# Layer 0's attention: clip and exponential over two blocks of keys at once, weighted blocks written in a row

## What is computed

```python
kc = k.reshape(B, H, Nc, CHUNK, Dh)          # CHUNK = 128, Nc = 8
vc = v.reshape(B, H, Nc, CHUNK, Dh)
scores = jnp.einsum('bhnd,bhjcd->bhnjc', q, kc) / jnp.sqrt(jnp.asarray(Dh, dtype=q.dtype))
scores = jnp.clip(scores, -10.0, 10.0)
scores = jnp.where(mask == 0, jnp.asarray(-10.0, scores.dtype), scores)
attn = jax.nn.softmax(scores, axis=-1)       # over the 128 keys of one block
ctx = jnp.einsum('bhnjc,bhjcd->bhnd', attn, vc)
```

## Time and profile before

| | |
|---|---|
| median of 3 runs | 3406.07 us (3404.3 to 3408.29) |
| profiled execution | 3398.74 us |
| its span | 3397.1 us |
| busy share of PE, DVE, ACT, POOL | 70%, 72%, 44%, 61% |
| mean granted TensorE clock | 0.822 of full |

### The profile page before, as it was taken

One profiled execution on the slowest core, in us unless ns is written; L12 is line 12 of the kernel. 1 busy time (PEld: TensorE's weight loads), 2 busy tenths in 40 slices (PEclk: granted clock), 3 DMA queues, 4 the chain that ended last, 5 costly groups with the idle time before them and its releaser, 6 DMA issues. The chain is left out here.

```text
span 3397.1 us, 91971 instructions
## 1 busy us (share of the span) xinstructions
PE 2366.9 (70%) x32653; PEld 1654.5 (49%) x32988; DVE 2435.1 (72%) x5337; ACT 1499.6 (44%) x2211; POOL 2056.8 (61%) x1733
## 2 busy tenths in 40 slices
PE   4488878785435888888885638885647777777760
PEld 2266666564322554554554526774425555555550
DVE  3399999897665877777784546535768888888856
ACT  2355555552221444444342324442336666666650
POOL 2387878783222655555564325552239999989971
PEclk8688888886666999999997768886669988889885
DMA  6732233222543222122114531203421212112215
GB/s 215 255 92 69 68 73 79 68 55 48 158 146 110 55 54 55 45 51 55 43 43 113 163 120 58 79 20 102 123 89 57 70 53 68 55 54 68 62 41 124
DMA packets 259867, 285.00 MB, mean 84 GB/s; under 512 B 147889, under 2 KB 211953, under 8 KB 259457
## 3 DMA queue, kind: packets, MB, share of 16 engines
q1 hardware_dynamic: 254848, 262.48, 26.9%
q0 software_dynamic: 4608, 16.78, 1.4%
HBM read 183.52 MB, written 95.36 MB: 82 GB/s over the span
## 5 line engine op out<-in xcount | busy, mean ns | idle before, releaser
L314 POOL TENSOR_TENSOR xg<-xc 128x512 f16<-128x512 f32 x1536 | 1813.0, 1206 | 671.8 <-ACT xc L788 556.7
L1009 PE MATMUL ps<-vs,xc 128*128 128x33 bf16 (+1 forms) x13824 | 850.3, 189 | 176.6 <-DVE work L1348 89.5
L1009 PEld LDWEIGHTS ps<-vs,xc 128*128 128x128 bf16 x13824 | 683.1, 101 | 501.6 <-issue 258.1
L1009 PE MATMUL ps<-vs,xg 128*128 128x33 bf16 (+1 forms) x9216 | 779.0, 187 | 0.3 <-issue 0.3
L1009 PEld LDWEIGHTS ps<-vs,xg 128*128 128x128 f16 x9216 | 596.9, 99 | 3.7 <-issue 3.7
L1290 DVE CUSTOM_DVE_ANT_0 full<-ks,mask_n 128x1024 bf16<-128x1024 f32 x320 | 456.4, 1426 | 69.5 <-DVE xn L1385 28.1
L788 ACT ACTIVATE xc<-ps 128x512 f32<-128x512 f32 x512 | 305.7, 597 | 438.9 <-PE ps L953 438.8
L788 ACT ACTIVATE xc<-cv,lift 128x512 f32<-128x512 f32 x512 | 350.4, 718 | 291.4 <-DVE cv L1323 290.1
L1300 DVE CUSTOM_DVE_ANT_0 full<-ps,mask_n 128x512 bf16<-128x512 f32 x512 | 353.0, 689 | 169.3 <-DVE top L1300 62.0
L968 PE MATMUL ps<-qs,sel 128*128 128x512 f32 x640 | 424.3, 665 | 0.2 <-ACT ps L767 0.2
L788 ACT ACTIVATE xc<-cv,cols 128x512 f32<-128x512 f32 x320 | 231.3, 723 | 383.1 <-DVE cv L1331 374.5
(11 more groups left out here) (136 smaller groups left out, 3540.6 us busy)
## 6 DMA issues: line engine op xcount, KB each, us to landing
qs<-q_d SPq DMA_DIRECT2D x224, 128.0 KB
ks<-k_d SPq DMA_DIRECT2D x224, 128.0 KB
ks<-row_d SPq DMA_DIRECT2D x40, 512.0 KB
part<-row_d SPq DMA_DIRECT2D x40, 512.0 KB
v_d<-vbuf SPq DMA_DIRECT2D x24, 792.0 KB, 4.2
vs<-v_d SPq DMA_DIRECT2D x96, 198.0 KB
q_d<-part SPq DMA_DIRECT2D x32, 512.0 KB
k_d<-part SPq DMA_DIRECT2D x32, 512.0 KB
```

The lines of the kernel that those rows point to most:

```text
L314: eng.tensor_tensor(plo[:, r, :], prob[:, r, :], phi[:, r, :], ALU.subtract).then_inc(low_done(layer, u, s)[0], 1)
L1009: mm = pe.matmul(acc, half[:, r, it * P:(it + 1) * P], vs[:, n, at:at + width], start=opens and h == 0 and v == 0, stop=h == 1 and v == 1, ...
```

## The change

In layer 0, the clip, the mask and the exponential are done for two neighbouring tiles in one operation over 2 x 512 columns. `settle_two(s)`, for even s, waits for both scores and writes two slots of `arg`; `exp_two(s)` reads them and writes two slots of `prob`, and raises `s_exp` by 2. `s_p` now counts pairs in layer 0, and all counts against it are adjusted, as are PE's waits ahead of an even score. The order of PE's loop, its wait for `s_chfree`, POOL's operations and the place of `blocks_done` in DVE's loop stay.

`blk`, the view of `work` into which the multiplication writes and from which the reduction reads, is laid out anew: before, the block j was the fastest index (step of one element), after, j is the slowest (step of 128 elements) and the 128 results of a block lie in a row.

```diff
-        blk = work[:, :, :].rearrange("p t f -> p (t f)").rearrange("p (t d j) -> p j t d", d=32, j=BLOCKS)
+        blk = work[:, :, :].rearrange("p j (t d) -> p j t d", d=32)
...
             if layer == 0:
-                return u * (TILES * UNROLL) + s
+                return u * (TILES // 2 * UNROLL) + s // 2
...
+                    def exp_two(s):
+                        T, r = tile_value(s), s % DEEP
+                        act.wait_ge(s_p, p_at(s))
+
+                        act.wait_ge(s_av, T - DEEP + 2)
+                        act.activation(prob[:, r:r + 2, :], arg[:, r % RING:r % RING + 2, :], ACT.Exp,
+                                       scale=2.0 * CLIP, bias=lift[:, 0:1]).then_inc(s_exp, 2)
...
-                        exps(s)
+                        if layer:
+                            exps(s)
+                        elif s % 2 == 0:
+                            exp_two(s)
...
                             if layer == 0:
-                                if not (first and s < RING):
-                                    pe.wait_ge(s_p, T - CREDIT - RING + 1)
+                                if s % 2 == 0 and not (first and s < RING):
+                                    pe.wait_ge(s_p, settled_before(layer, u, s - RING) + 1)
                                 mm = pe.matmul(bank, ks[:, n, blk_j], qs[:, n, cut], start=True, stop=True)
...
+                    def settle_two(s):
+
+                        T, r = tile_value(s), s % RING
+                        c, j = s // BLOCKS % 2, s % BLOCKS
+                        dve.wait_ge(s_score, T - CREDIT + 2)
+                        dve.wait_ge(s_exp, T - RING + 2)
+                        dve.scalar_tensor_tensor(arg[:, r:r + 2, :], ps[:, r:r + 2, :], -0.5,
+                                                 mask_t[:, j:j + 2, c * HALF:(c + 1) * HALF], ALU.max, ALU.min
+                                                 ).then_inc(s_p, 1)
...
-                        if s < total and layer != 1 and s % RING not in RELU_AT[layer]:
+                        if layer == 0 and s < total and s % 2 == 0:
+                            settle_two(s)
+                        if layer > 1 and s < total and s % RING not in RELU_AT[layer]:
                             settle(s)
```

## The result

The changed kernel takes 3693.1 us (median; 3688.5 to 3694.7) against 3407.2 for the kernel before: ratio 1.0838, 95% interval 1.0825 to 1.0851. The forecast was 3654 with a range of 3600 to 3712. It is slower by 286 us where 248 were forecast. In the profiled execution the span is 3686.9 us, 289.8 more than before. The stage of layer 0's attention, from the first clip to the operation on the mask that follows the last reduction, went from 632 us (164.4 to 796.6) to 910 (166.3 to 1075.9), +277. What follows it went from 2600.5 to 2611.0, and the stage begins 2 us later.

The account below looks back on a forecast made before the run. DVE was taken to bound layer 0's attention, PE close; the change closes a loop between them. 251 pairs x 3.32 + 62 reductions x 0.54 = 867 us against 618, +248: 3654 us, range 3600 to 3712.

Parts of the forecast that it names:

- The wait for two scores (1): In layer 0, the odd score waits behind a weighing needing DVE's last multiplication: PE and DVE loop once a pair.
- PE's part of the loop: From multiplication's end through weighing and odd score to the clip: 1.26 us at full clock, 1.67 at half.
- Clip, multiplication (2, 3): On DVE: clip over 1024 columns 1.22 us, 1.14 until the reciprocal; multiplication with contiguous output 0.43 instead of 0.64.
- Rival C: Multiplication stays at 0.64 us, 53 us more, 3707; or reduction stays near 1.22, 3624; chance 0.09 for either.
- Reduction (4): DVE's reduction, now reading with a step of 128 elements, goes from 1.220 to 1.90 us, once in four pairs.
- excess over PE's part: DVE's 2.05 us around the reduction outlasts PE's path by 0.79 us at full or 0.38 at half clock.
- ACT and POOL (5): Merged exponential and POOL's subtractions end about 4.7 us after the clip began, needed after over 9: covered, priced at nothing.
- The sum (6): Layer 0's loop: 3.07 us a pair at full clock, 3.48 at half, 3.32 mixed; stage 867 us against 618.
- the mixed clock: TensorE in the loop at granted clock 0.70, 60% of the time at half clock: 3654 us, chance 0.56.
- rival B: The same PE and DVE loop at half clock throughout: 897 us for the pairs, +279, 3685 us; chance 0.14.
- Rival D: Odd score gets out ahead of the weighing, no loop binds, DVE's total decides: -27 us, 3379 us; chance 0.05.

Follow-up runs that it names:

- filler run: The changed kernel plus two unread products of 512 columns once a pair, ahead of PE's waiting weighing: 3632.5 us, ratio 1.0663 to the kernel before.

## Why the prediction was right, point by point

**The wait for two scores (1).** Right in mechanism and place. PE's part of the loop, worked out as 1.26 us at full and 1.67 at half clock, is 1.25 in the filler run and 1.62 here. The half-clock weighing took 0.59 when it came out of an idle stretch (505.65 to 506.24), not 0.64.

**Clip, multiplication (2, 3).** 1.22 and 1.14 until the reciprocal: measured 1.225 and 1.14. Multiplication 0.43: measured 0.424. Rival C, that it stays at 0.64, fell. The clip's line of the page, with the mean in ns and the idle before it:

```profile
L1329 DVE SCALAR_TENSOR_TENSOR cv<-ps,mask_t 128x1024 f32<-128x1024 f32 x256 | 313.5, 1225 | 333.9 <-PE ps L957 311.7
```

**Reduction (4).** 1.90 forecast from L1213, 1.968 measured; 0.07 short. The excess over PE's part was put at 0.38 at half clock and is 4.02 - 3.41 = 0.61: 0.07 from the duration, 0.05 because PE's part is shorter, and the rest from what lies around the reduction, 0.03 ahead and 0.22 behind, 0.25 where 0.15 had been taken.

**ACT and POOL (5).** Covered, as said: the run with the exponential alone is equal to before, and POOL is 56 to 59% busy in the windows from 200 to 1000 us, where near 60% was forecast.

**The sum (6), and the step that missed.** The full-clock pair was 3.07, measured 3.04; the half-clock pair 3.48, measured 3.41. What was wrong is "60% of the time at half clock", taken from projection stretches with PE 58 to 68% busy at 0.64 and 0.74. Here PE is 71 to 74% busy in every window of 100 us from 200 to 1000, more than in either, and the clock is 0.50 throughout. The filler run has the same busy share, 71.7%, and 0.91. So the busy share in the windows was no guide from one stage to another. PE's share itself was put at up to 70% and its idle stretch at 1.1 to 1.4 us; the profile shows 0.84, since it counts the last score to its end (0.77 us) and not to where the next product could start.

So the forecast's own choice, the mixed clock with a chance of 0.56, did not come true, and the range was right because it took in rival B, half clock throughout, with 0.14. B gave 3685 against 3693. Over the same 251 pairs that the sum counts, the traces have 618.4 us before and 892.2 after (first multiplication at 175.39, the one of iteration 510 at 1067.59), where B had 897 and the forecast 867. That B came so close is in part luck: its pair was 0.07 too long, 18 us in all, and its excess for the reduction 0.23 too short, 14 us.

The sentence "neither engine can run ahead, whatever the durations are" is borne out by the filler run: with the clock nearly full the loop is intact. Rival D, faster by DVE's total, failed at the point that was named for it. The runs with four banks show that its sum would have failed with the loop open as well. Like is compared with like there: four banks with the whole change take 3390.0 us, four banks without it 3379.3. The change costs 11 us (6 to 9 against each chip's kernel before), where DVE's total gave a gain of 27; with both scores first too it comes to 3376.0, 3 us under.

**What the sum left out.** The start of the stage, until DVE's first multiplication, grew by 3 us (5.8 to 9.0) where the prediction had start and tail change by under 1. A further 10 us of the 290 in the profiled execution lie after the stage, in code that is the same but for counts; between the first and the last product of layer 1's line L920 (L928 in the changed kernel) 5.5 of them arise. Over all traces of this study that rest is 2600 to 2606 us in the four kernels that clip block by block, 2606 to 2612 in the nine that clip by pairs, and 2597 in the filler run, which clips by pairs too. Each is one execution, and the 7 to 13 executions of the kernel before on one chip lie 10 to 11 us apart, so this order may be chance; no run tests it, and its cause stays open.

## What to carry to other kernels

Before an operation is widened to take two inputs, walk back from the second input in its producer's queue: if anything ahead of it waits for work that the consumer does just before the widened operation, the two engines take turns, and here a saving of 0.06 us a pair cost 1.10 (14.25 against 9.85 us for four pairs). More buffers at that wait (two more banks for the weighted sums) were worth more than the other order of PE or the wider clip: 303 us with the change and 24 without it. And a new layout is a trade: time both its writer and its reader, and see which of them stops the others.

## What the runs showed of the hardware

- On DVE, 256 results of 32 bits written 32 bytes apart took 0.622 us, in a row 0.424 (mean of 256, with the old layout and in the changed kernel). A reduction that reads 1024 of them 512 bytes apart took 1.968 us against 1.220 in a row (mean of 64). The rule of 16-byte lines cited ahead of the result (the Trainium skill, SBUF — State Buffer, section on the DMA port swizzle) has the right sign in both; it gives no figure.
- TensorE stayed at 1.2 GHz from 200 to 1000 us, within the stage, with an idle stretch of 0.84 us in a pair of 3.41. Two products of 512 columns more in each pair brought the granted clock to 0.91 in the window shown (0.84 to 0.92 in those from 200 to 1000 us) and the stage from 910 to 862 us, though the profile's busy share did not change. The line that DVE's copy out of PSUM does not break PE's warmth (the Trainium skill, TensorE: Matmul & The Clock Gate, section on loop structure) does not carry over to this stage, in which PE waits for DVE's multiplication out of PSUM once a pair.
